# A decoder kernel whose top-32 attention marks the kept keys by ranks instead of by replaced scores

## The reference

```python
def _L3_attn_ref(x, Wq, bq, Wk, bk, Wv, bv, Wo, bo):
    B, S, E, H, K = (2, 256, 128, 16, 32)
    ...
    scores = jnp.einsum('bhsd,bhtd->bhst', q, k) / scale
    kk = min(K, s)
    top_s, top_i = jax.lax.top_k(scores, kk)
    probs = jax.nn.softmax(top_s, axis=-1)
    gather = jax.vmap(jax.vmap(lambda vv, ii: vv[ii]))
    v_g = gather(v, top_i)
    out = jnp.einsum('bhsk,bhskd->bhsd', probs, v_g)
    out = out.transpose(0, 2, 1, 3).reshape(b, s, e)
    return out @ Wo.T + bo
```

## Time and profile before

| | us |
|---|---|
| median of three runs | 2575.7 |
| time of the profiled execution | 2576.89 |
| its span in the profile | 2575.1 |
| the touched stage, first row maximum to its last addition | 1583.3 to 2352.4 |
| PE / DVE / ACT / POOL busy in the whole span | 1896.7 / 1757.7 / 1153.4 / 707.1 |

### The profile page before, as it was taken

One profiled execution on the slowest core, in us unless ns is written; L12 is line 12 of the kernel. 1 busy time (PEld: TensorE's weight loads), 2 busy tenths in 40 slices (PEclk: granted clock), 3 DMA queues, 4 the chain that ended last, 5 costly groups with the idle time before them and its releaser, 6 DMA issues. The chain is left out here.

```text
span 2575.1 us, 35710 instructions
## 1 busy us (share of the span) xinstructions
PE 1896.7 (74%) x11191; PEld 1097.5 (43%) x11203; DVE 1757.7 (68%) x5539; ACT 1153.4 (45%) x3171; POOL 707.1 (27%) x612
## 2 busy tenths in 40 slices
PE   5996889844868999969987876565655565556777
PEld 2644347442445666644453553233333333333343
DVE  5236342277765656647756567999999999995655
ACT  3653442242315666641143563555454555554412
POOL 1200045014432333310032320344333333331130
PEclk7988899965988999979988897666666666666978
DMA  5000100400000000000010000000000000000000
GB/s 204 2 1 1 36 18 31 158 1 1 2 1 1 2 1 0 0 1 0 30 65 1 1 1 0 1 1 1 1 1 1 1 1 1 1 1 0 1 0 17
DMA packets 10586, 37.70 MB, mean 15 GB/s; under 512 B 1344, under 2 KB 7488, under 8 KB 9136
## 3 DMA queue, kind: packets, MB, share of 16 engines
q1 hardware_dynamic: 8880, 33.06, 3.3%
q0 software_dynamic: 1536, 2.59, 0.3%
HBM read 30.18 MB, written 5.51 MB: 14 GB/s over the span
## 5 line engine op out<-in xcount | busy, mean ns | idle before, releaser
L3640 PE MATMUL psum<-work 32*128 32x256 f32 x512 | 129.1, 648 | 293.8 <-ACT work L3750 293.8
L3809 DVE MATCH_REPLACE8 work<-work 128x256 f32<-128x256 f32 x768 | 305.4, 408 | 0.0
L3857 POOL TENSOR_TENSOR work<-work 128x1024 f32<-128x1024 f32 x64 | 150.6, 2354 | 494.6 <-ACT work L3750 494.6
L3806 DVE MAX8 work<-work 128x8 f32<-128x256 f32 x768 | 266.6, 409 | 0.0
L3640 PEld LDWEIGHTS psum<-work 32*128 32x128 f32 x512 | 76.9, 308 | 319.3 <-ACT work L3750 161.1
L674 POOL TENSOR_TENSOR work<-work 128x256 f32<-128x256 f32 (+2 forms) x144 | 133.3, 944 | 265.5 <-DVE work L934 265.5
L864 ACT ACTIVATE work<-work 128x128 f32<-128x128 f32 (+1 forms) x320 | 144.9, 454 | 42.1 <-PE psum L734 25.4
L335 DVE RECIPROCAL work<-work 128x256 f32<-128x256 f32 x36 | 62.8, 1749 | 112.1 <-ACT work L405 111.9
L3750 ACT ACTIVATE work<-work 128x256 f32<-128x256 f32 x256 | 128.4, 501 | 0.0
L3663 PE MATMUL psum<-work,tiles 128*8 128x256 f32 x512 | 117.0, 609 | 13.9 <-ACT work L3759 13.9
L3859 POOL TENSOR_TENSOR work<-work 128x1024 f32<-128x1024 f32 x64 | 121.1, 1892 | 6.1 <-DVE work L3831 1.2
(11 more groups left out here) (620 smaller groups left out, 4632.4 us busy)
## 6 DMA issues: line engine op xcount, KB each, us to landing
big_weights<-L0f_dram SPq DMA_DIRECT2D x1, 6117.5 KB, 27.9
big_weights<-L_dram SPq DMA_DIRECT2D x1, 5892.0 KB, 16.8
big_weights<-L_dram SPq DMA_DIRECT2D x1, 4952.5 KB, 16.9
big_weights<-L_dram SPq DMA_DIRECT2D x1, 2091.0 KB, 21.4
choice_rows<-tiles SPq DMA_DIRECT2D x2, 1024.0 KB, 10.2
tiles<-choice_rows SPq DMA_DIRECT2D x8, 256.0 KB, 5.2
big_weights<-L_dram SPq DMA_DIRECT2D x1, 1630.5 KB, 13.9
big_weights<-L0f_dram SPq DMA_DIRECT2D x1, 1630.5 KB, 6.2
```

The lines of the kernel that those rows point to most:

```text
L3640: mm = nc.tensor.matmul(scores(n)[:, u, :], qb[head, tile % 2, u % 2 * P:(u % 2 + 1) * P], kb[head, tile % 2, :], start=True, stop=True, t ...
L3806: ch.step(v.max(top8[:, n % 2, u, r, :], src[:, u, :]))
L3809: ins = v.match_replace(raw[:, n % 2, u, :], top8[:, n % 2, u, r, :], src[:, u, :], REPLACED)
L3857: ch.link(g.tensor_tensor(mine, mine, rest[:, n % 2], ALU.subtract))
```

## The change

Three things change in `topk_attention`; everything else stays.

1. Scores are copied from PSUM to SBUF (`keep_scores`, into `kept`), a group ahead of their use; VectorE and ScalarE read the copy.
2. VectorE makes four `v.max` rounds but only three `v.match_replace` rounds. The replaced row is no longer needed. ScalarE instead compares every score with the 32nd largest (`compare`, giving signs -1, 0, 1 and their row sum in bf16), TensorE turns the signs (`turn_signs`), ScalarE squares them (`square`), and TensorE sums them up with a table of prefixes to a number for each key (`rank`). ScalarE takes these to SBUF (`keep_ranks`), and GpSimd clips them to 0 or 1 and multiplies them into the probabilities (`pick`). The sum of the 32 exponentials is made by GpSimd (`centre_few`, `add_few`) with one exponential on ScalarE (`sum_few`).
3. The inverted sums are no longer multiplied into the probabilities. GpSimd writes them into four scaled identities (`scale_ident`), and `turn` is a product with these, not a transposition.

```diff
             def score(n):
...
-                if n >= 2:
-                    pe.wait_ge(c.probs_ready.sem, c.probs_ready.at(n - 1))
+                if n >= 1:
+                    pe.wait_ge(scores_kept.sem, scores_kept.at(n))
...
+            def turn_signs(n):
+                pe.wait_ge(signs_ready.sem, signs_ready.at(n + 1))
...
+                    pe.wait_ge(ranks_kept.sem, ranks_kept.at(n))
                 for kt in range(2):
...
+                    for u in range(U):
+                        mm = nc.tensor.transpose(signs_t[:, kt, u, :], signs[:, n % 2, u, kt * P:(kt + 1) * P], ident16)
+                mm.then_inc(signs_turned.sem, 1)
+
+            def rank(n):
+                z = n % 2
+                pe.wait_ge(squares_kept.sem, squares_kept.at(n + 1))
+                for half in range(2):
+                    nc.tensor.matmul(bank(2 + half), far, signs[:, z, 2 * half:2 * half + 2, :].rearrange("p u k -> p (u k)"),
+                                     start=True, stop=False)
+                    for u in (2 * half, 2 * half + 1):
+                        nc.tensor.matmul(order[:, u, :], one_row[0:1, :], place_row[0:1, :], start=False, stop=False)
+                        for kt in range(2):
+                            mm = nc.tensor.matmul(order[:, u, :], squares[:, z, kt, u, :], prefix[:, kt, :], start=False,
+                                                  stop=(kt == 1 and u % 2 == 1))
+                mm.then_inc(ranks_ready.sem, 1)
...
-                            mm = nc.tensor.transpose(bank(4 + head)[:, at:at + P],
-                                                     probs[:, n % 2, 2 * head + q, kt * P:(kt + 1) * P], ident)
+                            mm = nc.tensor.matmul(bank(4 + head)[:, at:at + P],
+                                                  picked[:, n % 2, 2 * head + q, kt * P:(kt + 1) * P],
+                                                  scaled_ident[:, n % 2, 2 * head + q, :], start=True, stop=True)
                 mm.then_inc(c.probs_turned.sem, 1)
...
+            for t in range(GROUPS + 5):
...
                 if 0 <= t - 2 < GROUPS:
+                    turn(t - 2)
+                if 0 <= t - 1 < GROUPS:
+                    turn_signs(t - 1)
+                if t + 2 < GROUPS:
+                    score(t + 2)
+                if t % 2 == 1 and (t + 3) // 2 < TILES:
+                    project((t + 3) // 2)
+                if 0 <= t - 1 < GROUPS:
+                    rank(t - 1)
+                if 0 <= t - 2 < GROUPS:
                     mix(t - 2)
...
+            def compare(n):
...
+                    ins = nc.scalar.activation(signs[:, s, u, :], kept[:, s, u, :], ACT.Sign, scale=-1.0,
+                                               bias=top8[:, s, u, LAST, 7:8], accum_out=balance[:, s, u:u + 1])
+                ins.then_inc(signs_ready.sem, 1)
...
+            def square(n):
+                act.wait_ge(signs_turned.sem, signs_turned.at(n + 1))
+                nc.scalar.activation(squares[:, n % 2].rearrange("p t u q -> p (t u q)"),
+                                     signs_t.rearrange("p t u q -> p (t u q)"), ACT.Square).then_inc(squares_kept.sem, 1)
+
+            def keep_ranks(n):
+                act.wait_ge(ranks_ready.sem, ranks_ready.at(n + 1))
...
+                for u in range(U):
+                    ins = nc.scalar.activation(ranks[:, u, :], order[:, u, :], ACT.Relu, scale=2.0,
+                                               bias=balance[:, n % 2, u:u + 1])
+                ins.then_inc(ranks_kept.sem, 1)
...
                 if 0 <= t - 1 < GROUPS:
-                    soften(t - 1)
+                    compare(t - 1)
+                    sum_few(t - 1)
+                if t + 1 < GROUPS:
+                    keep_scores(t + 1)
+                if 0 <= t - 1 < GROUPS:
+                    square(t - 1)
+                if t < GROUPS:
+                    soften(t)
+                if 0 <= t - 1 < GROUPS:
+                    keep_ranks(t - 1)
+                if t % 2 == 1 and (t + 3) // 2 < TILES:
+                    take_queries((t + 3) // 2)
                 if 0 <= t - 2 < GROUPS:
                     take_turned(t - 2)
...
+                if r == LAST:
+                    return
...
             def pick(n):
-                mine = probs[:, n % 2]
                 pool.wait_ge(c.probs_ready.sem, c.probs_ready.at(n + 1))
-                ch.link(g.tensor_tensor(mine, mine, rest[:, n % 2], ALU.subtract))
-                pool.wait_ge(c.sums_inverted.sem, c.sums_inverted.at(n + 1))
-                g.tensor_tensor(mine, mine, rsum[:, n % 2, :].unsqueeze(2).broadcast_to([P, U, S]), ALU.mult) \
-                    .then_inc(c.probs_picked.sem, 1)
+                pool.wait_ge(ranks_kept.sem, ranks_kept.at(n + 1))
...
+                ch.link(g.tensor_scalar(ranks, ranks, 1.0, 0.0, ALU.min, ALU.max))
+                g.tensor_tensor(picked[:, n % 2], probs[:, n % 2], ranks, ALU.mult).then_inc(c.probs_picked.sem, 1)
```

More of the change, by code:

```diff
@@ L3579, in topk_attention @@
     NG, GROUPS, TILES = H // 2, B * H // 2, B * H // 4
+    LAST = K // 8 - 1
     a = Arena(c)
     qb, kb = a.take(2, S), a.take(2, S)
-    probs, rest, raw = a.take(2, U, S), a.take(2, U, S), a.take(2, U, S)
+    probs, raw = a.take(2, U, S), a.take(U, S)
+    ranks, picked = a.take(U, S), a.take(2, U, S)
+    signs = a.take(2, U, S // 2).bitcast(BF16)
+    squares = a.take(2 * U * S // 2).bitcast(BF16).rearrange("p (z t u q) -> p z t u q", z=2, t=2, u=U)
     turned = a.take(2, 2, 2, S)
@@ L3613, in piece_at @@
     def piece_at(t):
-        return t // 2 if t % 2 and t // 2 < PIECES else None
+        return t // 2 if t % 2 == 0 and t // 2 < PIECES else None
     with nc.Block() as block:
@@ L3705, in _ @@
             score(0)
+            project(1)
             make_values(1)
             make_values(2)
-            for t in range(GROUPS + 3):
-                if t + 1 < GROUPS:
-                    score(t + 1)
-                if t % 2 == 0 and t // 2 + 1 < TILES:
-                    project(t // 2 + 1)
+            score(1)
+            for t in range(GROUPS + 5):
                 if t == 0:
@@ L3734, in take_queries, with keep_scores @@
                                      bias=bq[:, tile % 4:tile % 4 + 1]).then_inc(c.qk_taken.sem, 1)
+            def keep_scores(n):
+                act.wait_ge(c.scores_ready.sem, c.scores_ready.at(n + 1))
+                if n >= 2:
+                    act.wait_ge(signs_ready.sem, signs_ready.at(n - 1))
+                    act.wait_ge(c.scores_masked.sem, c.scores_masked.at(n - 1))
+                for half in range(2):
+                    ins = nc.scalar.copy(kept[:, n % 2, 2 * half:2 * half + 2, :].rearrange("p u k -> p (u k)"), bank(half))
+                ins.then_inc(scores_kept.sem, 1)
@@ L3802, in choose @@
             def choose(n, r):
[L3803 removed]
+                src = kept[:, n % 2] if r == 0 else raw
                 for u in range(U):
[L3805 to L3810 removed]
+                    if r == 1 and u == U - 1:
+                        dve.wait_ge(c.scores_masked.sem, c.scores_masked.at(n + 1))
+                    else:
+                        ch.all_but(U - 2 if r == 1 else U - 1)
+                    ins = v.max(top8[:, n % 2, u, r, :], src[:, u, :])
+                    if r == LAST and u == U - 1:
                         ins.then_inc(c.scores_max.sem, 1)
@@ L3813, in choose, with invert @@
                         ch.step(ins)
+                if r == LAST:
+                    return
+                for u in range(U):
+                    ch.all_but(U - 1)
+                    ins = v.match_replace(raw[:, u, :], top8[:, n % 2, u, r, :], src[:, u, :], REPLACED)
+                    if r == 0 and u == U - 1:
+                        ins.then_inc(c.scores_masked.sem, 1)
+                    else:
+                        ch.step(ins)
+            def invert(n):
+                dve.wait_ge(c.kept_summed.sem, c.kept_summed.at(n + 1))
+                if n >= 2:
+                    dve.wait_ge(scaled_ready.sem, scaled_ready.at(n - 1))
+                v.reciprocal(rsum[:, n % 2, :], sums[:, n % 2, :]).then_inc(c.sums_inverted.sem, 1)
             def take_values(n):
@@ L3854, in pick, with scale_ident @@
+            def scale_ident(n):
+                s = n % 2
+                pool.wait_ge(c.sums_inverted.sem, c.sums_inverted.at(n + 1))
+                if n >= 2:
+                    pool.wait_ge(c.probs_turned.sem, c.probs_turned.at(n - 1))
+                for u in range(U):
+                    ins = g.tensor_scalar(scaled_ident[:, s, u, :], ident, rsum[:, s, u:u + 1], 0.0, ALU.mult, ALU.add)
+                ins.then_inc(scaled_ready.sem, 1)
             def pick(n):
-                mine = probs[:, n % 2]
@@ L3875, in mask_context @@
                     ch.link(g.tensor_tensor(x, x, c.w("L3x_vmask").unsqueeze(1).broadcast_to([P, CH // P, P]), ALU.mult))
-            for t in range(GROUPS + 4):
+            tables()
```

(11 more changed lines are left out.)

160 lines of the change are left out of this document (96 added, 64 removed).

## The result

| | before | after |
|---|---|---|
| median, us | 2579.39 (2575.64 to 2584.17, 4 runs) | 2752.85 (2749.07 to 2753.69, 4 runs) |
| ratio | | 1.0664, 95% interval 1.0638 to 1.0689 |
| span of the profiled execution | 2575.1 | 2751.6 |
| DVE / ACT / POOL busy in the span | 1757.7 / 1153.4 / 707.1 | 1660.2 / 1344.3 / 846.8 |

The change costs 6.6%. The prediction said 2710 us with a range of 2610 to 2810.

What follows compares the result with a forecast made beforehand. It took a dependence loop through GpSimd, TensorE and ScalarE to replace VectorE as bound: 63 loops of 13.4 us with start and tail gave +111, `put_out` 14 and context projections 8 more, +133 on 2576.9, so 2710 us, range 2610 to 2810.

Steps and rivals of the forecast that it cites:

- The ring: Between groups, `rank(n+1)` waits through `square`, `turn_signs`, `turn(n)`, `pick(n)` for `keep_ranks(n)`; the sum, 13.4 us, is paid every group.
- The walk: Step times added from one `keep_ranks` to the next; cold bursts gave 13.3 us, or 14.3 with `project`, mean 13.8.
- 85 in 100 bursts cold: Share of TensorE bursts starting at 1.2 GHz; 0.85 x 13.8 + 0.15 x 11.35 = 13.4 us a group.
- P: Time of one loop from group to group in the stage, put at 13.4 us; no difference at 11.63.
- `put_out` 14 us in all: On TensorE, `put_out` delays `turn` by about 2 us in 7 groups, its 8 records following a cold `mix`.
- The start: Copies, VectorE's rounds, then signs, turn, square, rank and ranks before the first loop; first ranks kept near 1603.
- The tail: End of the stage behind the 63 loops: 10.4 us from `turn`, 1.9 more for `turn`, 3.7 for `pick`, 16 in all.
- The 8 us for the context's projections: On TensorE at the end of `mix`, these projections delay the loop by 1.1 us in each of 7 groups.
- stayed up: Rival: TensorE's clock stays at 2.4 GHz, 11.35 us a group, 2567 us, a little faster or no change; chance 0.10.
- stayed down through `rank`: Rival: TensorE's clock stays at 1.2 GHz through `rank`, 16.7 us a group, 2918 us; chance 0.07.
- The costlier `turn`: Rival: `turn` without transpose mode costs four times its time, as the skill page says; +80 us, 2790; chance 0.03.
- VectorE is not the bound: Denies the rival that VectorE stays the bound, ring open or under 10.05 us, stage 100 us shorter, 2480; chance 0.05.

Runs made afterwards that it cites:

- two_clips: GpSimd clips the ranks twice in a row, the second clip changing nothing, against the changed kernel; 2822.33 us, 69.5 us more.
- fourth_match: The changed kernel with VectorE's fourth `match_replace` round put back, its result read by nobody; 2746.79 us, ratio 1.0673 to the kernel before.
- filled_pause: The changed kernel with 24 unread bf16 products filling TensorE's pause behind `rank` in every second group from the 18th; 2700.49 us, 52 us less.
- few_late_all: Changed kernel with TensorE order `turn_signs`, `rank`, `turn`, `score`, `project`, `mix`, the 32 exponentials' sums on ScalarE, queries taken behind `square`; 2665.21 us, 1.031 to before.
- turned_later: On top of few_late_all, ScalarE copies turned blocks a group later, behind `square`, and takes a sequence's output later; `mix` follows; 2599.90 us, 1.0076 to before.
- scale_in_clip: Changed kernel with inverted sums multiplied in by four GpSimd clips of 256, no scaled identities, `turn` a transposition again; 2943.97 us, ratio 1.1429 to before.
- late_score: The changed kernel with TensorE's `score` and `project` moved behind `rank`, and `turn` in their place; 2769.07 us, ratio 1.0759 to the kernel before.

## Why the prediction was right

**The ring.** The prediction's central step, that VectorE's bound is replaced by `turn`, `turn_signs`, `square`, `score`, `rank`, `keep_ranks`, `pick`, was right, and is shown from two sides: a microsecond added to `pick` comes out 64 times (two_clips), 1.6 us added to VectorE not once (fourth_match). So the 100 us that one match round is worth while VectorE is the bound are not there to gain, and the stage pays for the ring's length instead. In the groups with `put_out` the wait runs through ScalarE's program instead, a path that the prediction didn't have.

**Length of the ring.** The walk gave 13.3 and 14.3 us for cold bursts; 13.1 to 13.4 and 14.2 to 14.35 were measured. Most parts held: `turn` 16 records and 3.78 us (3.9 said), 1.14 for `score` and 1.03 for the squares. The clip is 1.04 us (1.17 said). Two did not, and that their sum came out is luck: the clock had risen 3.6 us after the start of `turn`, where 5.2 was taken, so that `score` was done 0.7 to 0.9 us earlier than walked; and `rank` took 2.75 us where the rows had been added up to 2.0, 0.7 us more.

**Mis-sized terms**, which together make 2753 out of 2710:
- *85 in 100 bursts cold.* In the steady part all are: from the 20th group on every `turn` not behind `put_out` takes 3.5 to 3.8 us. (Among the first 14 it took 1.95 to 3.8.) The two kinds of group take 13.2 and 14.27 us, so P without `put_out` is 13.73 instead of 13.4: 63 x 0.33, some 21 us.
- *`put_out` 14 us in all.* The seven groups with it in the loop take 20.44, five times 17.04, and 16.09 where their kind takes 14.27, together 22: 8 more. Its products run right behind a cold `mix` at 3.78 us. `turn` waits for them but is then only 2.21 us long; what holds the group up is that ScalarE takes their result ahead of `compare`.
- *The start.* The first ranks were kept at 1619.5, not 1603: 16.5 us. The stage itself began 4 us later than before. In it, `compare(0)` waits for the context's copy, which ScalarE's program has ahead of it, and the first `rank` is cold.
- *The tail.* From the last clip to the end of the stage 13.2 us pass, not 16: 3 less.
- 21 + 8 + 16.5 - 3 is 42.5 us, against the 43.5 from 2709.9 to the 2753.4 of the profiled execution. The clip's gain is inside the first of them. The 8 us for the context's projections held: 7.4 measured over the first 20 groups.

**The rivals.** The clock never stayed up and never stayed down through `rank` in the steady part. The costlier `turn` did not come: 3.78 us. VectorE is not the bound (fourth_match).

**Causes of the loss.** The ring comes from the order in which the work is written, the clock makes it longer, and undoing one of them alone gives back only a part or nothing. filled_pause gives back 52 of 173 us. The order without either ring (few_late_all, with the sums moved too) gives back 88, and with `take_turned` off the wait (turned_later) 153. That last kernel is still 0.8% slower than before, so no version shown here turns the saved match round into time.

## What to carry to other kernels

When work is taken from the bounding engine and given to three others, walk the new dependences through each engine's program order until you are back at the start: a ring over groups has no slack, however idle its engines are. Opening one ring shows only the next one, so walk them all before moving a step; here there were three, of about 14, 13.7 and 11.7 us. And a step that waits for another engine belongs in an engine's program where that other is long done, a group later if need be.

## What the runs showed of the hardware

- On GpSimd, a pass with two constants over 1024 fp32 elements takes 1.04 us, but four over 256 with a factor from a column of SBUF take 4.50 (scale_in_clip): 4.4 ns an element against 1.0. With constants, 256 elements took 0.40. The same passes over 128 elements with a factor (`scale_ident`) take 1.43 for four.
- TensorE's granted clock falls behind several short pauses too, none of them above 2 us, and in the middle of a burst (late_score, few_late_all). A pause of 2.56 us alone had left it up before the change. The Trainium skill ("TensorE: Matmul & The Clock Gate", "A second HAM failure mode: psum-queue depth-cycling") tells of frequent short idling between groups of products that makes the clock oscillate; the three windows of few_late_all, 1.00, 0.50 and 1.00, agree with it.
